# Attention of a twelve-stage model on one core: router moved between the first score maxima, token sums taken by ScalarE, the first split shared by two engines, expert weights loaded at the stage's start

## What is computed

```python
def _L3_ffn_ref(x, ...):                       # B=8, T=256, D=128, H=16, M=2 attention experts, E=8, K=2
    n1 = _ln(x, ln1_g, ln1_b)
    mha_probs = softmax(mean(n1, axis=1) @ mha_rw + mha_rb)              # the router: a weight per batch and expert
    q, kk, v = (einsum('btd,mdhk->mbhtk', n1, w) + b for w, b in ...)
    attn = softmax(einsum('mbhtk,mbhsk->mbhts', q, kk) / sqrt(KD))
    mha_out = einsum('mbtd..', attn @ v, mha_wo) + mha_bo
    x = x + einsum('mbtd,bm->btd', mha_out, mha_probs)
    n2 = _ln(x, ln2_g, ln2_b)
    ...                                        # top 2 of 8 feed-forward experts by a second router
```

## Time and profile before

| | before |
|---|---|
| median of 3 runs | 1878.57 us (1877.64 to 1880.87) |
| the profiled execution's own time | 1873.64 us |
| its span, first to last instruction | 1871.9 us |
| TensorE matmul busy | 1628.6 us (87%) |
| VectorE busy | 1278.7 us (68%) |
| ScalarE busy | 1163.1 us (62%) |
| GpSimd busy | 590.2 us (32%) |
| mean granted TensorE clock | 0.956 of full |
| L1 attention, first instructions of GpSimd | at 892.2 us |
| the two L3 layers, start | at 1232.5 and 1570.0 us |

### The profile page before, as it was taken

The page is one execution under the profiler, slowest core; times in us unless marked ns, Lnnn a source line. Parts: engine busy times, 40 slices in busy tenths (PEclk is TensorE's granted clock), DMA queues, the critical chain, the costliest instruction groups (busy, mean ns, idle before and its releaser), DMA issues.

```text
span 1871.9 us, 40552 instructions
## 1 busy us (share of the span) xinstructions
PE 1628.6 (87%) x15460; PEld 865.6 (46%) x15460; DVE 1278.7 (68%) x2625; ACT 1163.1 (62%) x2729; POOL 590.2 (32%) x739
## 2 busy tenths in 40 slices
PE   6999989898898989889588965869899997799998
PEld 2556355633456345633244322324455462355546
DVE  5875687546786488647475668547788764788876
ACT  4666466643666566646266664464788766388875
POOL 3651265202653065300474004223233101332310
PEclk9999999999999999999689988996999999699999
DMA  5000000000000000000541000015653100554410
GB/s 199 19 19 7 6 19 19 7 0 1 19 19 13 0 19 19 14 1 0 102 89 28 1 1 0 1 35 102 133 99 94 19 1 6 115 94 101 90 30 23
DMA packets 53870, 73.31 MB, mean 39 GB/s; under 512 B 5616, under 2 KB 38608, under 8 KB 53168
## 3 DMA queue, kind: packets, MB, share of 16 engines
q1 hardware_dynamic: 53680, 70.73, 17.2%
HBM read 44.46 MB, written 16.88 MB: 33 GB/s over the span
## 4 chain that ended last, share of the span: by engine, by line
PE 56%; ACT 14%; DVE 12%; issue 8%; POOL 6%; DMA 2%; DVEq 0%; SPq 0%; POOLq 0%; ACTq 0%
PE ps L197 52%; ACT arena L709 6%; DVE arena L801 2%; DVE arena L845 2%; ACT arena L1614 2%; PE ps L588 1%; ACT arena L270 1%; ACT arena L272 1%; POOL arena L945 1%; PE ps L1508 1%; DMA arena<-arena 1%; DVE arena L933 1%; POOL arena L944 1%; ACT arena L265 1%; DVE arena L1654 1%
## 5 line engine op out<-in xcount | busy, mean ns | idle before, releaser
L197 PE MATMUL ps<-arena 32*64 32x128 f32 (+7 forms) x10984 | 650.9, 302 | 57.8 <-ACT arena L1614 18.8
L197 PEld LDWEIGHTS ps<-arena 32*64 32x64 f32 (+4 forms) x10984 | 364.6, 118 | 340.7 <-issue 118.1
L197 PE MATMUL ps<-arena,w_L0f 128*128 128x512 f32 (+3 forms) x992 | 369.0, 507 | 31.1 <-DVEq L2835 9.3
L1614 ACT ACTIVATE arena<-ps 128x512 f32<-128x512 f32 (+1 forms) x640 | 333.3, 576 | 84.6 <-PE ps L197 76.1
L1654 DVE TENSOR_REDUCE arena<-ps 128x2 f32<-128x512 f32 x512 | 322.9, 684 | 87.4 <-PE ps L197 85.4
L709 ACT ACTIVATE arena<-ps,arena 128x128 f32<-128x128 f32 x512 | 226.7, 461 | 68.3 <-DVE arena L847 66.7
L197 PEld LDWEIGHTS ps<-arena,w_L0f 128*128 128x128 f32 (+2 forms) x992 | 174.6, 188 | 158.4 <-issue 98.9
L197 PE MATMUL ps<-arena,const 128*128 128x512 f32 (+2 forms) x532 | 171.8, 608 | 62.2 <-DVE arena L2136 22.1
L952 POOL TENSOR_TENSOR arena<-arena 128x512 f32<-128x512 f32 x128 | 132.5, 1042 | 154.8 <-DVE arena L831 154.5
L801 DVE TENSOR_TENSOR arena<-ps,arena 128x1024 f32<-128x1024 f32 x128 | 151.8, 1205 | 14.8 <-ACT arena L723 9.2
L723 ACT ACTIVATE arena<-ps 128x512 f32<-128x512 f32 x128 | 76.8, 600 | 100.4 <-DVE arena L801 77.7
(11 more groups left out here) (252 smaller groups left out, 2114.8 us busy)
## 6 DMA issues: line engine op xcount, KB each, us to landing
scratch<-arena SPq DMA_DIRECT2D x40, 384.0 KB, 2.8
arena<-scratch SPq DMA_DIRECT2D x80, 192.0 KB
arena<-scratch SPq DMA_DIRECT2D x80, 128.0 KB
arena<-arena SPq DMA_DIRECT2D x64, 128.0 KB, 2.4
arena<-scratch SPq DMA_DIRECT2D x80, 88.0 KB
...
```

Source lines behind the costliest of these rows:

```text
L197: return self.nc.tensor.matmul(o, lhsT, rhs, start=start, stop=stop, skip_group_check=True)
L1614: S.activation(self.pt[g % 4][:, e, 0:both], ps[:, self.shifted_bank(2 * g + e), 0:both], ACT.Exp, scale=self.scale).then_inc(self.exped.s ...
```

## The change

- **Expert weights.** The 8 transfers are issued at the start of the L3 stage, ahead of anything else on SyncE.
- **First split.** For unit 0 alone, in L1 and L3, the q half is split by VectorE and the k half by GpSimd at the same time (`cut`). SyncE writes plane pairs in three transfers, each as soon as both engines have made it, and reads in reverse order: the 11 and 16 row reads wait for the first two writes only, the 24 row reads for the third too.
- **Second norm.** VectorE keeps the product (`gain`); the addition of the shift goes to ScalarE, two instructions of 256 columns a chunk, whose accumulator output gives the token sums (`shift`). The four L2271 sums and four L282 additions leave VectorE. The means and projections on TensorE change places with each other.
- **Router.** Its VectorE parts are done between the first maxima: means ahead of step 1's maximum, logits ahead of step 3's, normalising and the products ahead of step 6's, clearing of the bank ahead of step 8's. TensorE's product comes at step 3, ScalarE's exponential at step 4; the product uses bank 6 instead of 7. Unit 2's projection no longer waits for `prepared`.
- **Table load.** ScalarE's load of the ln/exp table at the start of L3 goes; one is added at the end of the scan stage between the two L3 layers.

```diff
@@ -1392,7 +1394,7 @@
-        self.parts_out = [self.sig(f"parts_out{i}", 16 * n) for i, n in enumerate(turns)]
+        self.parts_out = [self.sig(f"parts_out{i}", 16 * (n - (i == 0))) for i, n in enumerate(turns)]
...
@@ -1469,6 +1471,8 @@
+        if u == 2:
+            self.wait_ge(eng, self.cut_q, PARTS)
...
@@ -1476,16 +1480,14 @@
-            if s == 1 - 2 * HEADS:
-                self.route_tensor(eng)
             u = k + 2
             if i == (2 if u == 2 else 0) and self.is_unit(u) and u >= 2:
                 self.wait_ge(eng, self.v_copied, k)
                 self.wait_ge(eng, self.ctx_copied, k - 3)
                 self.wait_out(eng, k - 4)
-                if u == 2:
-                    self.wait_prepared(eng)
                 self.project(eng, u)
+            if s == 3:
+                self.route_tensor(eng)
...
@@ -1582,11 +1584,11 @@
-            if s == 1 - 2 * HEADS:
-                self.route_scalar(eng)
             u = k + 2
             if i == (2 if u == 2 else 0) and self.is_unit(u) and u >= 2:
                 self.bias(eng, u)
+            if s == 4:
+                self.route_scalar(eng)
...
+            if k == 0:
+                self.route_vector(eng, ch, s)
...
-            if i == (2 if u == 2 else 0) and self.is_unit(u):
+            if i == 0 and u == 0:
+                self.cut(eng, ch, G, 1)
+            if i == (2 if u == 2 else 0) and self.is_unit(u) and u:
                 qk = self.qk[u % 2]
                 self.wait_ge(eng, self.biased, u + 1)
-                if u:
-                    out = self.parts_out[(u - 1) % self.STACKS]
-                    eng.wait_ge(out.sem, out.at(16 * ((u - 1) // self.STACKS + 1)))
+                self.wait_out_of(eng, u - 1)
                 ch.did(G.tensor_copy(self.part(0), qk))
                 ch.wait_ge()
...
+    def wait_out_of(self, eng, u):
+
+        i, out = u % self.STACKS, self.parts_out[u % self.STACKS]
+        if u == 0:
+            for first in self.first_out:
+                eng.wait_ge(first.sem, first.at(16))
+        else:
+            eng.wait_ge(out.sem, out.at(16 * (u // self.STACKS + (i > 0))))
+
+    def cut(self, eng, ch, E, y):
+
+        qk, rest, cut = self.qk[0][:, y, :], self.rest[:, y, :], (self.cut_q, self.cut_k)[y]
+        at = [(a, 2 * PARTS - 1 - a)[y] for a in range(PARTS)]
+        self.wait_ge(eng, self.biased, 1)
+        E.tensor_copy(self.parts[:, at[0], :], qk).then_inc(cut.sem, 1)
+        self.wait_ge(eng, cut, 1)
+        ch.did(E.tensor_tensor(rest, qk, self.parts[:, at[0], :], ALU.subtract))
+        ch.wait_ge()
+        E.tensor_copy(self.parts[:, at[1], :], rest).then_inc(cut.sem, 1)
+        self.wait_ge(eng, cut, 2)
+        o = E.tensor_tensor(self.parts[:, at[2], :], rest, self.parts[:, at[1], :], ALU.subtract)
+        o.then_inc((self.cut_q, self.low)[y].sem, 1)
+
...
     def sync(self, eng):
         U = self.units
+        if self.tail is not None:
+            self.tail.load(eng)
         for k in range(-2, U + 1):
             u = k - 1
-                self.wait_ge(eng, self.low, u + 1)
                 if turn:
                     eng.wait_ge(stacked.sem, stacked.at(16 * self.loads * turn))
-                eng.dma_start(scratch[0:2 * PARTS].rearrange("a p s -> p a s"), self.parts).then_inc(out.sem, 16)
-                eng.wait_ge(out.sem, out.at(16 * (turn + 1)))
+                if u == 0:
+                    for a in range(PARTS):
+                        self.wait_ge(eng, self.cut_q, a + 1)
+                        self.wait_ge(eng, *((self.low, 1) if a == PARTS - 1 else (self.cut_k, a + 1)))
+                        z = slice(a, 2 * PARTS - a, 2 * PARTS - 1 - 2 * a)
+                        eng.dma_start(scratch[z].rearrange("a p s -> p a s"), self.part(a)).then_inc(self.first_out[a].sem, 16)
+                else:
+                    self.wait_ge(eng, self.low, u + 1)
+                    eng.dma_start(scratch[0:2 * PARTS].rearrange("a p s -> p a s"), self.parts).then_inc(out.sem, 16)
+                    self.wait_out_of(eng, u)
...
-                for slot, n, apart in RUNS:
+                for slot, n, apart in reversed(RUNS) if u == 0 else RUNS:
+                    if u == 0:
+                        for first in self.first_out[0:PARTS if slot == 0 else PARTS - 1]:
+                            eng.wait_ge(first.sem, first.at(16))
                     for e in range(2):
                         row = 64 * e + KD * slot
                         pair = rows[e, 0:2 * apart].rearrange("(x r) c -> r x c", x=2)
                         eng.dma_start(to[row:row + n], pair[0:n]).then_inc(stacked.sem, 16)
-                if u == 5 and self.tail is not None:
-                    self.tail.load(eng)
...
         if self.ahead:
+            self.cut(eng, ch, self.k.nc.vector, 0)
             self.norm.finish(eng, ch, 3)
         else:
             self.norm.vector(eng, ch)
+            self.cut(eng, ch, self.k.nc.vector, 0)
...
+        S.preload_act_table_set("natural_log_exp_and_others")
...
+        self.router = Router(self, self.h, 0, M, self.mp, rep, mean, small, bank=6)
...
+
+    def shift(self, eng, c):
+
+        k, n = self.k, self.norm
+        self.wait_ge(eng, self.gained, c + 1)
+        for b in range(PER * c, PER * (c + 1)):
+            h = self.h[:, b * SEQ:(b + 1) * SEQ]
+            o = k.nc.scalar.activation(h, h, ACT.Identity, bias=k.C(n.shift), accum_out=self.mean[:, b:b + 1])
+        o.then_inc(n.done.sem, 1)
 
     def tensor(self, eng, ch):
         f, n = self.first, self.norm
@@ -2335,32 +2395,30 @@
         f.wait_done(eng, 0)
         n.center(0)
         f.center(3)
+        n.mean(eng, 0)
         f.mean(eng, 2)
-        n.mean(eng, 0)
         f.wait_done(eng, 1)
         n.center(1)
         f.mean(eng, 3)
         if self.r == 0:
             eng.wait_ge(self.k.loaded["L3m"], 16)
         self.project(eng, 0)
+        n.mean(eng, 1)
         f.wait_done(eng, 2)
         n.center(2)
-        n.mean(eng, 1)
+        n.mean(eng, 2)
         f.wait_done(eng, 3)
         n.center(3)
-        n.mean(eng, 2)
+        self.project(eng, 1)
         n.mean(eng, 3)
-        self.project(eng, 1)
-        n.wait_done(eng, 3)
+        n.wait_ge(eng, n.logged, 3)
         self.heads_tensor(eng)
 
     def route_tensor(self, eng):
-        self.wait_ge(eng, self.biased, 2)
         self.router.tensor(eng)
 
     def scalar(self, eng, ch):
         f, n = self.first, self.norm
-        self.k.nc.scalar.preload_act_table_set("natural_log_exp_and_others")
         f.square(eng, 0)
         f.square(eng, 1)
         f.invert(eng, 0)
@@ -2370,46 +2428,54 @@
         f.square(eng, 3)
         n.invert(eng, 0)
         f.invert(eng, 2)
+        self.shift(eng, 0)
+        n.square(eng, 1)
         self.bias(eng, 0)
-        n.square(eng, 1)
         f.invert(eng, 3)
         n.invert(eng, 1)
         n.square(eng, 2)
+        self.shift(eng, 1)
         n.invert(eng, 2)
         n.square(eng, 3)
+        self.bias(eng, 1)
         n.invert(eng, 3)
-        self.bias(eng, 1)
+        self.shift(eng, 2)
+        self.shift(eng, 3)
         self.heads_scalar(eng)
 
     def route_scalar(self, eng):
         self.router.scalar(eng)
 
     def vector(self, eng, ch):
-        k, V = self.k, self.k.nc.vector
-        f, n = self.first, self.norm
+        f = self.first
         f.finish(eng, ch, 0)
         f.finish(eng, ch, 1)
-        n.finish(eng, ch, 0)
+        self.gain(eng, 0)
         f.finish(eng, ch, 2)
+        self.cut(eng, ch, self.k.nc.vector, 0)
         f.finish(eng, ch, 3)
-        n.finish(eng, ch, 1)
-        self.router.sum_tokens(eng, ch, 0)
-        n.finish(eng, ch, 2)
-        self.router.sum_tokens(eng, ch, 1)
-        n.finish(eng, ch, 3)
-        self.router.sum_tokens(eng, ch, 2)
-        self.router.sum_tokens(eng, ch, 3)
-        n.wait_done(eng, 3)
-        self.router.vector(eng, ch)
-        mpv = self.mp.rearrange("p (b e) -> p b e", e=M_EXPERTS)
-        ch.did(V.tensor_scalar(self.bop, mpv[:, :, 0:1].rearrange("p b e -> p (b e)"), k.C("bo0"), None, ALU.mult))
-        ch.wait_ge()
-        V.scalar_tensor_tensor(self.bop, mpv[:, :, 1:2].rearrange("p b e -> p (b e)"), k.C("bo1"), self.bop, ALU.mult, ALU.add)
-        for m in range(M_EXPERTS):
-            o = V.tensor_scalar(self.bvp.rearrange("p (b e) -> p b e", e=M_EXPERTS)[:, :, m:m + 1], mpv[:, :, m:m + 1], k.C(f"vL3_{m}"), None, ALU.mult)
-        o.then_inc(self.prepared.sem, 1)
-        self.open_bank(eng)
+        for c in range(1, NCHUNK):
+            self.gain(eng, c)
         self.heads_vector(eng, ch)
+
+    def route_vector(self, eng, ch, s):
+        V = self.k.nc.vector
+        if s == 1:
+            self.norm.wait_done(eng, 3)
+            self.router.means(eng, ch)
+        if s == 3:
+            self.router.logits(eng, ch)
+        if s == 6:
+            self.router.normalise(eng, ch)
+            mpv = self.mp.rearrange("p (b e) -> p b e", e=M_EXPERTS)
```

(8 more changed lines are left out.)

11 lines of the change are left out of this document (10 added, 1 removed).

## The result

| | before | after |
|---|---|---|
| median of 13 runs | 1877.64 us (1873.69 to 1885.01) | 1862.18 us (1858.05 to 1871.60) |
| ratio of the two | | 0.9919, 95% interval 0.9903 to 0.9935 |
| profiled execution, its own time | 1873.64 us | 1865.16 us |
| its span | 1871.9 us | 1863.4 us |
| VectorE busy | 1278.7 us | 1277.5 us |

The account below looks back on a forecast made before the run. Stage starts were taken as bound by bias, split, write and reads, then VectorE's maxima. L1 -1.7, first L3 +0.6 and -5.2 for loads, second L3 +1.3: together -5.0 us, from 1878.57 to 1873.6 us; range 1868.9 to 1878.9.

Parts of the forecast that it names:

- Loads: First L3: issuing the expert loads at the stage's start cuts unit 3 to unit 4 from 18.91 to 13.72 us, -5.2 us.
- Second parts at B + 2.5, third at B + 3.6: First split, three stages: parts ready 2.5 and 3.6 us after B, the end of unit 0's bias, with engines hindering each other.
- The write takes 2.5 us: First split, three stages: a write of a third of the bytes takes 2.5 us, so first read at B + 5.0.
- Read to first score product, unchanged at 8.5: Three stage starts: first read to first score product stays at 8.58 and 8.44 us, since the bytes are the same.
- Router in the open, +2.75 a stage: Both L3: the router, before nearly hidden by the reads, delays VectorE's maxima by 2.75 us each, bounds 1.9 and 4.4.
- B in L3, +0.25 each: Both L3: the end of unit 0's bias comes 0.25 us later through ScalarE's shift, bounds -0.1 and +1.0.
- Costing nothing: the fewer VectorE additions and sums before the first product.: Before the first product: taking these off VectorE changes no time, because VectorE waits for ScalarE there.
- the one without hindrance: Rival: VectorE and GpSimd do not slow each other in splits and router, -3.7 us more, 1869.9 us; chance 0.17.
- The clock's 1.4 us a stage: Rival: TensorE's clock shifts each stage start by up to 1.4 us, giving 1870.8 or 1876.4 us; chance 0.17, half each.

Follow-up runs that it names:

- reads_old_order: The changed kernel with the first unit's reads in the old order: 1866.37 us, ratio to the kernel before 0.9950.
- router_ahead: The changed kernel with the router's steps back ahead of the maxima on all three engines: 1860.92 us, ratio to the kernel before 0.9921.
- gpsimd_alone: The changed kernel with GpSimd alone making the first split of all 512 columns, still in three writes: 1863.28 us, ratio to the kernel before 0.9922.
- rest_later: The changed kernel with four product operations and the bank's clearing moved from unit 0's maxima to unit 1's: 1864.05 us, ratio to the kernel before 0.9914.
- warm_fill: The changed kernel with products that nothing reads on TensorE while it waits for the first reads: 1862.00 us, ratio to the kernel before 0.9911.

## Why the prediction was wrong

The direction, the loads and the path were right, the sizes were not: the forecast's own sum, with measured terms in it, comes to -12.9 us instead of -5.0. By its steps:

- **Loads**, -5.2: measured 13.72 for 18.91 us in the trace, and 6 us as a kernel of its own. Right.
- **Second parts at B + 2.5, third at B + 3.6**: measured 1.9 and 2.8. I let VectorE delay GpSimd; in L1 it is VectorE that pays most (0.85 us for its subtraction, 0.50 in the second L3, where it starts ahead of GpSimd's), while GpSimd's 0.67 is about the 0.70 taken. The Trainium skill, SBUF — State Buffer, section Who interferes with whom, has the two exclude one another; the trace shows the longer operations, but two halves side by side end at B + 1.9, not at the B + 2.7 worked out from it.
- **The write takes 2.5 us**: 1.8. With the step before, the first read leaves at B + 3.8 instead of B + 5.0. This is the term that failed first: 1.2 us in each of three stages.
- **Read to first score product, unchanged at 8.5**: 7.7 to 8.1. I left it because the bytes are the same, and did not ask what their order does; in the old order, in reads_old_order, it is 9.0 to 9.2. These two terms are the largest miss: by the means the first score product follows B 3.8, 4.2 and 3.9 us sooner, where I had 1.7, 2.4 and 1.7 and as upper bounds 2.5, 3.2 and 2.5. That is 6.2 us over the three stages.
- **Router in the open, +2.75 a stage**: from first score product to first turn the L3 stages take 17.0 us in the mean of six, 15.1 in four of the kernel before: +1.9, my lower bound, and 1.7 us less for both than taken. And it is no cost against the alternative: in the second L3 of router_ahead it is VectorE that the first maximum waits for.
- **B in L3, +0.25 each**: +0.1 and +0.3 by the means. Right.
- **Sum.** L1 -3.8; first L3 -4.2 + 0.1 + 2.1 - 5.2; second L3 -3.9 + 0.3 + 1.7: -12.9 us. The measured ratio's interval is -12.2 to -18.2, so these terms suffice; the 2.6 us between -12.9 and the medians' -15.5 are not told from noise.
- **"Costing nothing: the fewer VectorE additions and sums before the first product."** This is no part of the missing time, since the changed kernel has both, but as a price it is wrong. I named ScalarE as their cover and did not ask what they cost once the first read leaves 2.9 us earlier and the first score product could go 3.9 us earlier. Without them, and what else of the L3 change goes with them, the split is worth nothing (1871.3 against 1870.3), with them about 9 us. A sum of separate prices has no place for two chains of which the later one counts; it came out here only because the change moves both.
- **Range.** Of the rivals, the one without hindrance had the right side, 1869.9, but I gave the reads no chance to come earlier than in it. The clock's 1.4 us a stage is real: B in the second L3 is 15.2 or 16.2 us from the start in unchanged code. Its part in the difference between kernels is open.

What stays open: what the parts bring only together, 9 or 10 us, has an interval of 4 to 17 us, and the stages of the single traces show it only to within their 2 to 3 us; which piece of the L3 change frees the split; and whether the clock's earlier return in the first L3 is cause or effect. No version beat the changed kernel: router_ahead, gpsimd_alone, rest_later and warm_fill equal it.
